# Router ahead of the rotations, group 0 without its trip through DRAM, second batch projected inside the feed-forward

## What is computed

```
xn = layernorm(x)
q, k, v = xn @ Wq.T, xn @ Wk.T, xn @ Wv.T        # 16 sub-heads of 8 for q, k; 8 heads of 16 for v
q, k = t*cos*s + rotate_half(t)*sin*s            # rotations by tables
probs = softmax(q k^T);  diff = probs[even] - lam * probs[odd];  attn = rms_norm(diff @ v) @ Wo.T
pooled = mean over tokens of xn;  h = tanh(pooled @ W1 + b1);  p = softmax(h @ W2 + b2)
w = top 3 of 8 zones of p, normalised            # the router, one choice for each batch
ffn = xn + sum over the 3 zones of w * gelu(xn @ Wa[zone]) @ Wb[zone]
out = x + attn + ffn
```

## Time and profile before

| | us |
|---|---|
| median of three runs | 469.81 (468.75 to 470.42) |
| the profiled execution, its own time | 470.11 |
| its span | 468.3 |
| what lies around the span | 1.81 |

### The profile page before, as it was taken

The page is one execution under the profiler, slowest core; times in us unless marked ns, Lnnn a source line. Parts: engine busy times, 40 slices in busy tenths (PEclk is TensorE's granted clock), DMA queues, the critical chain, the costliest instruction groups (busy, mean ns, idle before and its releaser), DMA issues.

```text
span 468.3 us, 7295 instructions
## 1 busy us (share of the span) xinstructions
PE 435.2 (93%) x2634; PEld 193.1 (41%) x2634; DVE 381.8 (82%) x720; ACT 338.1 (72%) x441; POOL 126.4 (27%) x146
## 2 busy tenths in 40 slices
PE   7797699999999799999999999999999999999987
PEld 5665455566656323323333333333333333332335
DVE  4855488998999779998999999999989998986225
ACT  2434454655655568889889988888889888989972
POOL 4153899887786200010000010001001001000000
PEclk9979899999999979999999999999999999999999
DMA  7826944110000220002001120000000000000003
GB/s 190 327 53 250 355 196 135 47 47 1 1 2 1 71 110 4 1 1 92 1 1 35 59 76 19 1 1 1 2 4 0 3 1 1 1 3 3 1 0 91
DMA packets 12182, 25.65 MB, mean 55 GB/s; under 512 B 1266, under 2 KB 6002, under 8 KB 11890
## 3 DMA queue, kind: packets, MB, share of 16 engines
q1 hardware_dynamic: 11456, 24.38, 15.0%
q10 hardware_dynamic: 690, 0.80, 0.7%
HBM read 15.48 MB, written 9.44 MB: 53 GB/s over the span
## 4 chain that ended last, share of the span: by engine, by line
PE 63%; ACT 9%; issue 9%; DVE 8%; DMA 5%; POOL 3%; SPq 2%; ACTq 0%; POOLq 0%
PE ps L1104 19%; PE ps L1074 16%; PE ps L1097 10%; ACT E L628 8%; DVE part_max L796 6%; PE ps L1036 3%; DMA q_scr<-ropeL 3%; PE ps L937 2%; PE ps L939 2%; PE ps L938 2%; PE ps L1037 2%; PE ps L1038 2%; DMA X<-in_x 1%; POOL hL L449 1%; SPq L306 1%
## 5 line engine op out<-in xcount | busy, mean ns | idle before, releaser
L796 DVE TENSOR_REDUCE part_max<-ps 128x1 f32<-128x512 f32 x512 | 319.2, 679 | 37.7 <-PE ps L1074 33.9
L628 ACT ACTIVATE E<-ps 128x1024 f32<-128x1024 f32 x256 | 246.0, 1027 | 38.0 <-PE ps L1097 37.2
L1104 PE MATMUL ps<-E,Vg 128*32 128x512 f32 x1024 | 138.1, 612 | 1.1 <-ACT E L628 1.1
L1074 PE MATMUL ps<-K,Q 32*128 32x512 f32 x384 | 111.0, 477 | 3.4 <-DVE part_max L796 2.8
L1097 PE MATMUL ps<-Q,K 32*128 32x512 f32 x384 | 89.0, 486 | 7.0 <-ACT E L628 5.3
L1074 PEld LDWEIGHTS ps<-K,Q 32*128 32x128 f32 x384 | 46.8, 184 | 93.4 <-DVE part_max L796 89.5
L449 POOL TENSOR_TENSOR hL<-h,hH 128x512 fp32r<-128x512 f32 x48 | 61.3, 1287 | 12.2 <-ACT hH L600 11.5
L598 ACT ACTIVATE h<-ps 128x512 f32<-128x512 f32 x48 | 28.6, 597 | 35.2 <-PE ps L939 21.8
L1097 PEld LDWEIGHTS ps<-Q,K 32*128 32x128 f32 x384 | 36.2, 184 | 37.3 <-ACT E L628 33.3
L495 POOL TENSOR_TENSOR U<-AT,rsum 128x256 f32<-128x256 f32 x15 | 9.3, 621 | 145.0 <-DVE rsum L851 136.2
L1104 PEld LDWEIGHTS ps<-E,Vg 128*32 128x32 f32 x1024 | 20.3, 108 | 38.4 <-issue 32.5
(11 more groups left out here) (144 smaller groups left out, 392.8 us busy)
## 6 DMA issues: line engine op xcount, KB each, us to landing
K<-k_scr SPq DMA_DIRECT2D x6, 512.0 KB, 3.9
Q<-q_scr SPq DMA_DIRECT2D x6, 512.0 KB, 4.9
tab<-in_tables SPq DMA_DIRECT2D x2, 1024.0 KB, 6.5
q_scr<-ropeH SPq DMA_DIRECT2D x4, 512.0 KB, 6.6
k_scr<-ropeH SPq DMA_DIRECT2D x4, 512.0 KB, 4.5
wa_raw<-in_wa SPq DMA_DIRECT2D x6, 256.0 KB, 2.7
wb_raw<-in_wb SPq DMA_DIRECT2D x6, 256.0 KB, 2.9
X<-in_x SPq DMA_DIRECT2D x2, 512.0 KB, 7.0
```

Of the source, the lines that this page charges most:

```text
L628: nc.scalar.activation(E[:, par, 2 * jj:2 * jj + 2, :].rearrange("p j t -> p (j t)"), ps[:, 2 * jj:2 * jj + 2, :].rearrange("p j t -> p (j ...
L796: nc.vector.tensor_reduce(part_max[:, tile // FC % 2, j * FC + tile % FC, sh:sh + 1], ps[:, SLOT_BANK[quad_slot(t) + k], :], AX.X, ALU.max ...
L1074: mm(ps[:, SLOT_BANK[x], :], Qs[g % KQ_BUFS][strip(j), tile % TB * P:(tile % TB + 1) * P], Ks[g % KQ_BUFS][strip(j), sh * BANK:(sh + 1) * ...
L1104: last = mm(ps[QUAD * j:QUAD * (j + 1), B_PV, :], Vg[:, par, st, j // 2, :], E[:, s % 2, k, :], start=(st == 0), stop=(st == TB - 1), skip ...
```

## The change

1. The router comes first. DVE normalises batch 1 before it rotates anything; the product for lambda is made between the two normalisations; SP reads the picks and loads the raw weights before it writes any rotated rows; the sums of the first batch's rotations (m = 0 to 3) move from POOL to DVE (`rope_sum`); ACT instead of POOL makes the first `waH`. The tables are issued without waiting for `X`.
2. Group 0's strips no longer go through DRAM: `strip_rows(m)` makes two matmuls with a 32 x 128 selection matrix (a new input of 64 KB), `strip_evacuate(m)` copies the result into `Q` and `K` of group 0.
3. `project(8)` to `project(15)` (batch 1) move into units 8, 10, ... 22 of the feed-forward, with their `rotary` halves on DVE; `values(2)`, `values(3)` and their transposes into units 0, 2, 4 and 6; `rope_add`, `rope_high`, `rope_low` of batch 1 follow in units 11 to 26; `start_sum(1)` moves into unit 1.
4. Bank 3 now holds those products, so the ring of the row maxima has three banks instead of four in units 0 to 25.
5. `zT` takes the place of `XN` in SBUF, and the copies into it no longer wait for the scratch writes. Four warming matmuls after `turn(1)` are gone.

What follows of a table, the numbers of `lead_ring`, stands in the first lines of the diff; the orders behind it show the instructions themselves.

```diff
-    return (4, 5, 2, 3) if n < 22 else (4, 5, 3, 0) if n < 26 else (4, 5, 0, 1)
+    return (4, 5, 2) if n < 22 else (4, 5, 0) if n < 26 else (4, 5, 0, 1)
...
+PROJ = ((0, 0), (1, 0), (1, 1), (0, 1), (0, 2), (0, 3), (1, 2), (1, 3))
+
+PROJ_BANK = ((4, 5), (6, 0), (1, 4), (5, 6))
+STRIP_BANK = (0, 0, 1, 1)
+
+X_BANK = 3
+V_BANK = (2, 3, X_BANK, X_BANK)
+BESIDE = {0: ("value", 2), 2: ("turn", 2), 4: ("value", 3), 6: ("turn", 3)}
+BESIDE.update({8 + 2 * k: ("project", 8 + k) for k in range(8)})
+
+
 def proj_bank(k):
 
-    return 4 + (k % 3 if k < 14 else k % 2)
+    return PROJ_BANK[k // 2][k % 2] if k < 8 else X_BANK
...
-            sp.wait_ge(x_in[1], 16)
             for kind in range(2):
                 sp.dma_start(tab[:, 2 * kind:2 * kind + 2, :], tables[:, 2 * kind:2 * kind + 2, :]).then_inc(tab_in[kind], 16)
...
+            sp.wait_ge(pick_done, 2)
+            zones = [picked(0)]
+            raw_load(0, zones[0])
+            zones += [picked(1)]
+            raw_load(1, zones[1])
+            scratch(1)
+            sp.wait_ge(scr_out, 48)
             scratch(0)
-            sp.wait_ge(scr_out, 48)
-            scratch(1)
-            sp.wait_ge(pick_done, 2)
-            zones = [picked(0), picked(1)]
-            raw_load(0, zones[0])
-            raw_load(1, zones[1])
...
             def wa_zone(e):
                 par = e % 2
-                pool.wait_ge(raw_in[par], 32 * (e // 2 + 1))
-                if e >= 2:
-                    pool.wait_ge(g1_done, UZ * (e - 1))
-                    pool.sem_inc(pool_waited, 1)
-                nc.gpsimd.tensor_copy(waH[:, par, :], wa_raw[:, par, :]).then_inc(wah_done, 1)
+                if e:
+                    pool.wait_ge(raw_in[par], 32 * (e // 2 + 1))
+                    if e >= 2:
+                        pool.wait_ge(g1_done, UZ * (e - 1))
+                        pool.sem_inc(pool_waited, 1)
+                    nc.gpsimd.tensor_copy(waH[:, par, :], wa_raw[:, par, :]).then_inc(wah_done, 1)
...
-            rope_add(0)
-            for m in range(1, 4):
-                rope_add(m)
-                rope_low(m - 1)
+            for m in range(3):
+                rope_low(m)
+            wa_zone(0)
             rope_low(3)
-            rope_add(4)
-            rope_low(4)
-            wa_zone(0)
-            rope_add(5)
-            rope_low(5)
-            wa_zone(1)
             wb_zone_low(0)
             for n in range(UNITS):
                 h_low(n)
-                if n in (3, 7):
-                    rope_add(6 + n // FC)
-                    rope_high(6 + n // FC)
-                    rope_low(6 + n // FC)
+                if n == 1:
+                    wa_zone(1)
+
+                if n in (11, 15, 19, 23):
+                    rope_add(4 + (n - 11) // 4)
+                if n in (14, 18, 22, 26):
+                    rope_low(4 + (n - 14) // 4)
...
+            def strip_evacuate(m):
+
+                kind, c = PROJ[m]
+                act.wait_ge(strip_ps, m + 1)
+                dst, src = (Qs, Ks)[kind][0][:, c * BANK:(c + 1) * BANK], ps[:, STRIP_BANK[m], :]
+                if kind:
+                    nc.scalar.activation(dst, src, ACT.Identity, bias=cst[:, C_K1:C_K1 + 1]).then_inc(strip_out, 1)
+                else:
+                    nc.scalar.activation(dst, src, ACT.Copy).then_inc(strip_out, 1)
...
-            nc.scalar.activation(identR[:], ident, ACT.Copy).then_inc(id_done, 1)
-            rope_high(4)
-            values_turn(2)
-            values_turn(3)
-            values_out(2)
-            values_out(3)
-            rope_high(5)
+            rope_high(2)
+            strip_evacuate(1)
+            rope_high(3)
+            act.wait_ge(raw_in[0], 32)
+            nc.scalar.activation(waH[:, 0, :], wa_raw[:, 0, :], ACT.Copy).then_inc(wah_done, 1)
+            strip_evacuate(2)
@@ -611,11 +628,20 @@
             wb_zone_high(0)
             for n in range(UNITS):
                 gelu(n)
+                if n == 0:
+                    strip_evacuate(3)
+
+                kind, at = BESIDE.get(n - 2, (None, 0))
+                if kind == "value":
+                    values_turn(at)
+                elif kind == "turn":
+                    values_out(at)
+                if n in (14, 18, 22, 26):
+                    rope_high(4 + (n - 14) // 4)
                 if n % UZ == 5 and n // UZ + 1 < PICKS:
...
+            def rope_sum(m):
+
+                dve.wait_ge(rot_done, 2 * (m + 1))
+                if m >= 2:
+                    dve.wait_ge(ropel_done, m - 1)
+                nc.vector.tensor_tensor(rope[:, m % 2, :], rot[:, m % ROT_BUFS, 0, :], rot[:, m % ROT_BUFS, 1, :],
+                                        ALU.add).then_inc(rope_done, 1)
+
             statistics(0)
             moments(0)
+            dve.wait_ge(s_in, 16 * 6)
+            nc.vector.tensor_tensor(lam_p[:], lam_in[:, 0:4:2], lam_in[:, 1:4:2], ALU.mult).then_inc(lam_prod, 1)
             normal(0)
             statistics(1)
             xn_low(0)
             moments(1)
             xn_low(1)
+            normal(1)
             rotary(0)
-            normal(1)
+            rope_sum(0)
+            xn_low(2)
             rotary(1)
-            xn_low(2)
             xn_low(3)
-            dve.wait_ge(s_in, 16 * 6)
-            nc.vector.tensor_tensor(lam_p[:], lam_in[:, 0:4:2], lam_in[:, 1:4:2], ALU.mult).then_inc(lam_prod, 1)
-            rotary(2)
+            rope_sum(1)
...
@@ -835,6 +870,9 @@
             for n in range(UNITS):
                 for t, k in lead_slots(n):
                     reduce_slot(t, k)
+                kind, at = BESIDE.get(n, (None, 0))
+                if kind == "project":
+                    rotary(at // 2, (at % 2,))
                 if n % UZ == 2 and n // UZ + 1 < PICKS:
...
                 m, r = k // 2, k % 2
-                kind, c = (m // CB) % 2, (m // (2 * CB)) * CB + m % CB
+                kind, c = PROJ[m]
                 pe.wait_ge(xl_done, c + 1)
-                if k >= 3:
-                    pe.wait_ge(rot_done, k - 2 + (k >= 14))
+                if 5 <= k < 8:
+                    pe.wait_ge(rot_done, k - 4)
+                elif k == 8:
+                    pe.wait_ge(v_out, CHUNKS)
+                elif k > 8:
+                    pe.wait_ge(rot_done, k)
                 t = slice(c * BANK, (c + 1) * BANK)
...
+            def strip_rows(m):
+
+                kind, c = PROJ[m]
+                pe.wait_ge(ropel_done, m + 1)
+                if m in (0, 2):
+                    pe.wait_ge(rot_done, 4 + m // 2)
+                else:
+                    pe.wait_ge(strip_out, m)
+                if m == 0:
+                    pe.wait_ge(sel_done, 1)
+                t = slice(c * BANK, (c + 1) * BANK)
+                mm(ps[:, STRIP_BANK[m], :], sel[:, 2 * kind, :], ropeH[0:QUAD, kind, t], start=True, stop=False)
+                mm(ps[:, STRIP_BANK[m], :], sel[:, 2 * kind + 1, :], ropeL[0:QUAD, kind, t], start=False,
+                   stop=True).then_inc(strip_ps, 1)
...
             turn(0)
             turn(1)
-            keep_warm(4)
+            pe.wait_ge(lam_prod, 1)
+            mm(ps[:, 3, 0:2], cst[0:DQ, C_ONE:C_ONE + P], lam_p[:], start=True, stop=True).then_inc(lam_ps, 1)
             pool_sums(0)
             pe.wait_ge(w_split, 1)
-            for k in range(4):
-                project(k)
+            project(0)
+            project(1)
+            project(2)
             turn(2)
+            project(3)
+            pe.wait_ge(lam_exp, 1)
             turn(3)
             pool_sums(1)
             project(4)
-            project(5)
             pe.wait_ge(pool_done, 1)
             pe.wait_ge(s_in, 16 * 6)
             mm(ps[0:ROUTER, 7, 8:8 + BATCH], w1_in[:], pooled[:], start=True, stop=True).then_inc(hid_ps, 1)
-            project(6)
-            pe.wait_ge(lam_prod, 1)
+            project(5)
             pe.wait_ge(hid_sb, 1)
-            project(7)
             values(0)
             values(1)
-            project(8)
-            project(9)
+            strip_rows(0)
+            project(6)
+            project(7)
...
-            pe.wait_ge(v_out, CB)
+            strip_rows(1)
+            strip_rows(2)
             pe.wait_ge(id_done, 1)
-            start_sum(0)
-            start_sum(1).then_inc(hs_free, H_BUFS)
+            pe.wait_ge(strip_out, 2)
+            start_sum(0).then_inc(hs_free, H_BUFS)
-            for k in range(13, 16):
-                project(k)
-            pe.wait_ge(rot_done, 12)
-            pe.wait_ge(v_out, CHUNKS)
+            pe.wait_ge(rot_done, 8)
             pe.wait_ge(wa_split, 1)
             first(0)
             pe.wait_ge(wbc_done, 1)
             first(1)
+            strip_rows(3)
             pe.wait_ge(gelu_done, 1)
             first(2)
...
             for n in range(UNITS):
+                if n == 1:
+                    pe.wait_ge(strip_out, 4)
+                    start_sum(1)
```

(14 more changed lines are left out.)

139 lines of the change are left out of this document (71 added, 68 removed).

## The result

The changed kernel takes 474.16 us (median of 8 runs, 472.54 to 476.34), the kernel before 470.04 (8 runs, 468.28 to 470.58): ratio 1.009, 95% interval 1.0068 to 1.0112. It is slower by 0.9%; the forecast was 465.3. The profiled execution took 472.54 (span 470.8), the fastest of its eight. The ratios leave out one slow execution, of experiment 6.

A forecast was written before the change was run, and what follows sets the result against it. PE was taken to bound the feed-forward, and a chain of waits over SP to hold the start. Start -14.5, added PE work +8.8, ring +3.2, stalls -2.0 make -4.5: 465.3 us, range 460 to 470.5.

The forecast's parts named there:

- (a): Prelude, first normalisation: xnL of chunk 1 ends at 15.75, 0.5 later, as lambda's product waits for six small loads.
- (b): Prelude: batch 1 is normalised at once, 2.3 with the reciprocal, so PE turns it at 18.05 instead of 21.38.
- (c): Prelude on PE: transposes, one projection and pooled sums at full clock end at 21.9, where it was 25.57.
- (d): Prelude, pooled sums to router's exponential: two projections (1.4) and six small operations (1.5), ending at 24.8.
- (e): Prelude, exponential to pick: 4.0 instead of 6.58, as two of three VectorE blocks and a rotation's tail go; 28.8.
- (g): Prelude behind the pick: VectorE's weights, rotations and additions, then ACT, then GpSimd's first waL at 36.8; weight transfer not last.
- (h): End of prelude: first(0) to first row maximum kept at about 5.2, so it starts at 42.0, 14.5 earlier.
- rival 1: Small loads come late behind the early tables, first normalisation 3 to 6 later: 468.3 to 471, taken at 468.5; chance 0.16.
- ring: Feed-forward, units 0 to 25: three banks instead of four cost 0.125 a unit, 3.2 us in all.
- Rival 2: Feed-forward, units 0 to 25: PE and VectorE take turns, 0.37 a unit, about 473 us; chance 0.09.
- Rival 4: Units 10 to 26: saturated GpSimd hands its stalls to PE (3 to 4 us), 469 us; chance 0.07.
- Rival 3: Feed-forward: the ring costs nothing and GpSimd's stalls all go, 461 us; chance 0.13.

The follow-up runs named there:

- experiment 6: Kernel of experiment 2 without the 24 projection matmuls of batch 1 in units 8 to 22 (result not valid): 464.4 us, ratio 0.9881.
- experiment 1: Changed kernel with one line back, so SP issues the tables only when X has landed: 467.6 us, ratio 0.995.
- experiment 2: Changed kernel with lambda's vector loaded first on ACT's queue under its own semaphore, tables still early: 467.24 us, ratio 0.9938.
- experiment 10: Kernel of experiment 7 plus 18 warming matmuls in PE's late gap: 464.85 us, ratio 0.9875.
- experiment 11: Kernel of experiment 10 with values, their transposes and projections between the second and third row-maximum product of their unit: 467.07 us, ratio 0.993.
- experiment 12: Kernel of experiment 10 plus four warming matmuls between the transposes and the pooled sums: 465.84 us, ratio 0.9917.
- experiment 3: Changed kernel with ten more warming matmuls on PE (40 instead of 30) at the start: 473.72 us, ratio 1.0054.
- experiment 8: Kernel of experiment 2 with SP writing batch 0's k rows before it reads the picks: 481.47 us, ratio 1.0229.
- experiment 7: Kernel of experiment 2 with the additions of m = 0 to 3 back on GpSimd: 465.45 us, ratio 0.9908.
- experiment 9: Kernel of experiment 2 with the four warming matmuls back between transposes and pooled sums: 468.07 us, ratio 0.9963.
- experiment 5: Kernel before the change with the row maxima's ring cut to three banks in units 0 to 25: 473.78 us, ratio 1.0096.

## Why the prediction was wrong, step by step

From the profiled executions, ends in us of the span:

| step | predicted | measured | own error |
|---|---|---|---|
| (a) `xnL` of chunk 1 | 15.75 | 18.66 | +2.9 |
| (b), (c) pooled sums of batch 1 | 21.9 | 28.26 | +3.45 |
| (d) router's exponential | 24.8 | 30.76 | -0.4 |
| (e) pick | 28.8 | 34.51 | -0.25 |
| (g) first `waL` | 36.8 | 42.41 | -0.1 |
| (h) first row maximum | 42.0 | 48.66 | +1.05 |

The steps that failed are (a) and (c), at the start of the prelude. The own errors add up to 6.65 of the 6.66 by which the first row maximum is late; with 0.4 more in the feed-forward that is about the distance of the profiled execution from its 465.6 (6.9).

(a) I priced the wait for six small loads at 0.5, because in the kernel before they had finished with X at 8.9. There the tables waited for X; here they were issued from 1.86 on, and each small packet had to take turns with a large one. The trace of before had a sign of it: 2 packets of ACT's queue in half a microsecond while X was moving. I had the mechanism as rival 1, with 3 to 6 us and a chance of 0.16. It came as 3.69, and experiments 1 and 2 show it by removing it in two ways. By the rule of the Trainium skill that was quoted there ("DMA: Bandwidth & Descriptors", section "Queues, rings and completion order": a DMA engine goes round its queues and drains a whole packet first) rival 1 would have been the forecast. The trace agrees with it in the microsecond that is shown, with 60 packets of one queue to 62 of the other.

(c) I took the full clock, since the idle time of 2.60 ahead of the transposes goes. The clock was 0.51 for ten microseconds, behind the 3.20 of idle time that the wait of (a) had put in another place. What was slow were the matmuls that stand in PE's list ahead of batch 1's transposes, for which step (c) has no term: batch 0's transposes 1.94 instead of 1.3, its pooled sums 3.57 instead of 1.84, three projections 3.98 instead of 2.1. Batch 1 could have been turned at about 20.9 (18.66 + 2.3) and was turned at 24.82; at full clock PE would have been there at about 20.6. So the 3.45 is this delay of 3.9, less 0.4 behind it. My own fallback had 2.7, near it by luck: it priced the pooled sums of batch 1 and the projections behind them, which then ran at full clock. The 1.05 of (h) is the clock once more, at 39.4 to 45.4: from `first(0)` to the first row maximum it was 6.1 here, and 4.8 where the clock stayed full (experiments 10 to 12).

Which idle time makes the clock fall isn't shown. In the profiled executions it fell before 20 us behind 3.20 and 2.03 of idle time (the changed kernel, experiment 3), but also behind 1.65, 1.54, 1.07, 0.88 and 0.18 (experiments 1, 2, 11, 8, 10), and it did not behind 0.29 to 1.54 in experiments 6, 7, 9 and 12 (a few matmul records may be missing, so some of these are upper bounds). All eight runs of the changed kernel have a mean clock of 0.968 to 0.975, those of experiment 2 have 0.977 to 0.985; so less clock goes with the wait, but only the profiled execution shows where. The median is 1.6 above that execution, whose mean clock is among the highest; where the others lost it no trace shows.

Rival 1 alone (468.5) would not have got there either: the late loads and the fallen clock add up on the chip, and were two separate "ifs" in the text. First reads tell them apart: 41.90 with the loads in time and no early fall (experiment 6), 44.98 with the early fall and a longer late one (experiment 2), 49.19 with late loads too. Of these last 4.2, experiment 2 has `XN` on PE 2.86 earlier; the other 1.4 falls to the clock, which is at half for longer early and for less time late in the changed kernel.

(d), (e), (g) were right within 0.4, and so were their reasons: one long VectorE instruction beside GpSimd's `ropeL` is left (1.30 against 0.21, for the same shape), the first weights (their second load issued at 36.00) are waited for by nobody, and the last chain is VectorE, ACT, GpSimd.

The feed-forward: +10.0 predicted, +10.4 measured (102.8 to 113.2). By stretches between the starts of `second`:

| units | before | after | more | by my terms |
|---|---|---|---|---|
| 0 to 8 | 18.28 | 20.57 | 2.3 | values, transposes, start sum 3.2, ring 1.0, stalls -2.0: 2.2 |
| 8 to 24 | 34.37 | 41.77 | 7.4 | projections 5.6, ring 2.0: 7.6 |
| 24 to 27 | 6.69 | 7.32 | 0.6 | ring 0.25 |
| 27 to 47 | 41.38 | 41.45 | 0.1 | 0 |

The sum is right, in part by luck: the terms are not additive as I wrote them. The ring alone costs 4.0, not 3.2 (experiment 5), 2.9 of it in units 8 to 24. With the projections' matmuls gone 39.58 of the 41.77 remain there (experiment 6), so they are worth 2.2 where I added 5.6. Without them PE is held up by other things, with intervals of 2.94 and 2.57 in which ACT and PE wait for GpSimd's `hL` behind an addition (read from the order in time, not tested); the projections otherwise cover these waits.

With the wait of (a) out the median is 467.24 (experiment 2), 1.9 over the forecast of 465.3; its fastest run, which has the highest clock, took 465.49. So the forecast's time is that of this kernel's best execution, not of its middle one.

Rival 2 (the ring serialises) didn't come: 0.22 a unit against its 0.37, and 4.0 in all against 9.6. Rival 4 (GpSimd hands its stalls to PE) didn't either: PE was busy for 47.14 of 48.00 in the middle. Rival 3 (the ring costs nothing) is out by the same 4.0.

No experiment took group 0's selections out by themselves, so what they give alone is not shown.

## What to carry to other kernels

Before an instruction moves ahead in an engine's list, look up what it waits for, and price that wait with the traffic that the same change puts beside it, not with the landing time of the old trace. Where a wait is moved to a place ahead of matmul work, allow for the clock in its price: 3.7 us of waiting cost 6.6 to 6.9 by medians. Redo the working of each step with what the engine still has ahead of it in its list, at half clock too. And when times of two versions differ by less than the clock's play within one version (here 3 to 5 us), compare runs of the same granted clock before you credit the edit; if the edit itself may move the clock, say so.
